# A fused attention and mixture-of-experts kernel: reordered prologue (second half's queries, a selector copy, a weight split, the load of batch 1)

## The reference, cut to what matters

```python
def block(x, ctx, g_xattn, g_ffn, weights):
    q = (layernorm(x) @ Wq.T).heads() / sqrt(16)
    k, v = (ctx @ Wk.T).heads(), (ctx @ Wv.T).heads()
    scores = q @ k.T + (q @ p_params)[clip(row - col, -4, 4) + 4]
    scores = where(row >= col, scores, -1e30)
    x = x + tanh(g_xattn) * (softmax(scores) @ v).merge() @ Wo.T
    x = x + tanh(g_ffn) * moe(layernorm(x))    # top 4 of 8 by groups, and a shared expert
    return x
```

## Time and profile before

| what | value |
|---|---|
| median of 3 runs | 638.78 us (636.84 to 639.2) |
| the profiled execution's own time | 637.0 us |
| its span, first to last instruction | 635.2 us |
| mean granted TensorE clock, share of full speed | 0.978 |
| TensorE matmul busy | 573.6 us, 90% of the span |
| VectorE busy | 420.9 us, 66% |
| ScalarE busy | 290.7 us, 46% |
| GpSimd busy | 197.0 us, 31% |

### The profile page before, as it was taken

How to read it: one execution, slowest core, us unless ns; L and a number is a source line. 1 busy time by engine, 2 the same in 40 slices (tenths; PEclk the granted TensorE clock), 3 DMA queues, 4 the chain that set the end, 5 groups by cost and what they waited for, 6 DMA issues and landing times.

```text
span 635.2 us, 10542 instructions
## 1 busy us (share of the span) xinstructions
PE 573.6 (90%) x3232; PEld 451.9 (71%) x3232; DVE 420.9 (66%) x884; ACT 290.7 (46%) x549; POOL 197.0 (31%) x199
## 2 busy tenths in 40 slices
PE   3647978899989999888989999999999999999997
PEld 3436745566557655544768888888888888888886
DVE  5396659875997688755777557466474754746454
ACT  3443578446855695477324342242423334233222
POOL 4155015500542045200123333224243242333223
PEclk9777999899999999999999999999999999999999
DMA  5883345435443535541510312203222032121320
GB/s 179 189 203 106 83 88 131 96 81 111 109 116 92 110 98 117 163 156 38 142 46 2 108 60 84 83 0 100 66 72 69 25 100 66 51 69 48 102 67 33
DMA packets 43585, 58.13 MB, mean 92 GB/s; under 512 B 8448, under 2 KB 25856, under 8 KB 43520
## 3 DMA queue, kind: packets, MB, share of 16 engines
q1 hardware_dynamic: 42464, 55.90, 32.4%
q10 hardware_dynamic: 1088, 1.84, 1.3%
HBM read 33.13 MB, written 6.11 MB: 62 GB/s over the span
## 4 chain that ended last, share of the span: by engine, by line
PE 74%; DVE 13%; issue 5%; ACT 3%; DMA 2%; SPq 1%; ACTq 1%; POOL 0%; DVEq 0%; POOLq 0%
PE py L1674 16%; PE pg L1658 16%; PE pu L1658 15%; PE smax L1010 4%; DVE mx L731 3%; PE oT L1077 3%; PE work L984 3%; PE work L1092 3%; PE oT L1081 3%; PE sT L1057 2%; DVE sx L746 2%; PE sT L1056 2%; PE pm L1628 1%; PE work L946 1%; PE pm L1620 1%
## 5 line engine op out<-in xcount | busy, mean ns | idle before, releaser
L1321 POOL TENSOR_TENSOR hl<-sg,hh 128x512 fp32r<-128x512 f32 x72 | 94.0, 1306 | 209.7 <-ACT hh L1366 209.7
L622 ACT ACTIVATE ex<-sT 128x512 f32<-128x512 f32 (+1 forms) x160 | 92.4, 593 | 75.1 <-PE sT L1057 53.3
L1360 ACT ACTIVATE sg<-pg 128x512 f32<-128x512 f32 x72 | 43.1, 598 | 181.6 <-PE pu L1658 181.5
L1674 PE MATMUL py<-split,hh 128*128 128x256 f32 x576 | 113.9, 282 | 0.1
L731 DVE TENSOR_REDUCE mx<-smax 128x2 f32<-128x308 f32 x187 | 81.1, 472 | 27.1 <-PE smax L1010 25.7
L1674 PEld LDWEIGHTS py<-split,hh 128*128 128x128 f32 x576 | 93.3, 189 | 3.9 <-issue 0.5
L1658 PE MATMUL pu<-x2h,split 128*128 128x512 f32 x288 | 90.5, 395 | 0.0
L1658 PE MATMUL pg<-x2h,split 128*128 128x512 f32 x288 | 90.3, 394 | 0.0
L1674 PE MATMUL py<-split,hl 128*128 128x256 f32 x288 | 80.6, 282 | 0.0
L1658 PEld LDWEIGHTS pu<-x2h,split 128*128 128x128 f32 x288 | 54.1, 188 | 13.0
L1500 DVE TENSOR_TENSOR sg<-cwb,sg 128x512 f32<-128x512 f32 x64 | 56.9, 891 | 8.9 <-DMA cwb<-cwt_d 6.3
(11 more groups left out here) (162 smaller groups left out, 953.1 us busy)
## 6 DMA issues: line engine op xcount, KB each, us to landing
cwb<-cwt_d SPq DMA_DIRECT2D x64, 256.0 KB, 3.4
qs<-qh SPq DMA_DIRECT2D x56, 128.0 KB, 2.5
ks<-km SPq DMA_DIRECT2D x16, 231.0 KB, 3.1
qs<-ql SPq DMA_DIRECT2D x28, 128.0 KB, 2.5
at<-rden_d SPq DMA_DIRECT2D x56, 64.0 KB, 2.3
out<-x SPq DMA_DIRECT2D x7, 512.0 KB, 4.5
wx<-in_wx SPq DMA_DIRECT2D x9, 384.0 KB, 7.4
x<-in_x SPq DMA_DIRECT2D x3, 1024.0 KB, 13.7
```

The lines of the kernel that those rows point to most:

```text
L622: nc.scalar.activation(ex[:, g % 2, i % 5, q0:HALF], ST[i % 2][:, q0:HALF], ACT.Exp).then_inc(exp_s, 1)
L1321: nc.gpsimd.tensor_tensor(hl[:, i % R, :], sg[:, i % R, :], hh[:, i % R, :], ALU.subtract).then_inc(hl_done, 1)
L1360: nc.scalar.activation(sg[:, i % R, :], PG[i % RG][:], ACT.Silu).then_inc(sg_s, 1)
L1674: return nc.tensor.matmul(PY[j // 2][:, (j % 2) * D:(j % 2 + 1) * D], ha[:, i % R, j * P:(j + 1) * P], wa[:, e, 2 * C * I:XW], start=first ...
```

## The change

Four pieces of the prologue change their place; no arithmetic is added or dropped.
- TensorE does the queries of half 1 after the 32 score products and `max_T` instead of ahead of them. `q_out` of half 1 (ScalarE), `q_lo` of half 1 (VectorE, after `tile0`) and the twelve DMAs of its rows follow. Each queue issues the four DMAs of the high parts once `q_hi` is 4, and the two of the low parts once `work_free` is 10.
- ScalarE's long selector copy goes between `x_hi` and `q_out` of half 0; the short ones go behind the `near` copies, and `m_row` goes ahead of `q_out` and `q_rows` of half 1.
- VectorE makes `wql` after the relative-position constants and the normalised x of half 0. TensorE's wait for `wq_set` stays where it is.
- SyncE issues the load of x of batch 1 ahead of the rows of half 1; those of batches 2 and 3 stay behind them.

```diff
--- before.py
+++ after.py
@@ -396,9 +396,11 @@
         sp.wait_ge(km_in, K_LOADS)
         for g in range(NG):
             k_stack(g)
-        sp.wait_ge(work_free, 9)
-        q_stack(1, 0)
         x_load(1)
+        sp.wait_ge(q_hi, 4)
+        q_stack(1, 0, (0, 2))
+        sp.wait_ge(work_free, 10)
+        q_stack(1, 0, (1,))
         for i in range(2, B):
             x_load(i)
         batches(sp, unit)
@@ -560,17 +562,20 @@
                                src[0:32, :, :].rearrange("p j d -> p (j d)").unsqueeze(1)
                                .broadcast_to([32, NSTK, 2 * DIST])).then_inc(const_set, 1)
 
-        def selectors():
+        def long_selectors():
 
             act.wait_ge(pool_set, 4)
+            nc.scalar.copy(ks[96:128, :, :].rearrange("p s (j k) -> p s j k", j=2),
+                           con("head", 96, 128).rearrange("p (s j) -> p s j", j=2).unsqueeze(3)
+                           .broadcast_to([32, NSTK, 2, KL])).then_inc(const_set, 1)
+
+        def short_selectors():
+
             for par in range(2):
                 nc.scalar.copy(k2[96:128, par::2, :].rearrange("p s (q k) -> p s q k", q=4)
                                [:, :, 2 * par:2 * par + 2, 0:K1],
                                con("head", 96, 128).rearrange("p (s j) -> p s j", j=2)[:, par::2, :].unsqueeze(3)
                                .broadcast_to([32, NG, 2, K1])).then_inc(const_set, 1)
-            nc.scalar.copy(ks[96:128, :, :].rearrange("p s (j k) -> p s j k", j=2),
-                           con("head", 96, 128).rearrange("p (s j) -> p s j", j=2).unsqueeze(3)
-                           .broadcast_to([32, NSTK, 2, KL])).then_inc(const_set, 1)
 
         def x_hi(u, use):
             for c in range(C):
@@ -652,20 +657,23 @@
         constants_late()
         k_hi(0, MAX_BANKS[0], True)
         x_hi(0, 0)
+        long_selectors()
         q_out(0, 2)
         act.wait_ge(work_free, 4)
         q_rows(act, 0, 1, range(3))
         x_hi(1, 5)
-        selectors()
+        for p in range(0, NM, 2):
+            near(0, p, M_START, True)
+        short_selectors()
+        for stk in range(1, NSTK):
+            m_row(0, 0, stk)
         for part in range(2):
             act.wait_ge(qs_in[0][part], 16 * 6)
-        q_out(1, 7)
-        for p in range(0, NM, 2):
-            near(0, p, M_START, True)
-        act.wait_ge(work_free, 9)
-        q_rows(act, 1, 1, range(3))
-        for stk in range(1, NSTK):
-            m_row(0, 0, stk)
+        q_out(1, 8)
+        act.wait_ge(q_hi, 4)
+        q_rows(act, 1, 1, (0, 2))
+        act.wait_ge(work_free, 10)
+        q_rows(act, 1, 1, (1,))
         batches(act, unit)
         raw_out(2 * B - 1, 1, 3)
 
@@ -876,8 +884,6 @@
         dve.wait_ge(x_first, 16)
         norm_stats(0, 0)
         dve.wait_ge(w_in, 5 * 16)
-        dve.wait_ge(wq_set, 1)
-        nc.vector.scalar_tensor_tensor(wql[:], wq, SCALE, wqh[:], ALU.mult, ALU.subtract).then_inc(wq_set, 1)
         nc.vector.tensor_scalar(reld[:], rel[:, DIST:2 * DIST], rel[:, 2 * DIST:], None, ALU.subtract)\
             .then_inc(rel_set, 1)
         dve.wait_ge(rel_set, 1)
@@ -888,6 +894,8 @@
         dve.wait_ge(rel_set, 2)
         nc.vector.tensor_tensor(rell[:], relm[:], relh[:], ALU.subtract).then_inc(rel_set, 1)
         normalised(0, 0, start=True)
+        dve.wait_ge(wq_set, 1)
+        nc.vector.scalar_tensor_tensor(wql[:], wq, SCALE, wqh[:], ALU.mult, ALU.subtract).then_inc(wq_set, 1)
         k_lo(0, MAX_BANKS[0])
         x_lo(0, 0)
         dve.wait_ge(x_in[0], 16)
@@ -896,15 +904,15 @@
         normalised(0, 1)
         v_in(0, 4, True)
         x_lo(1, 5)
-        q_lo(1, 7)
         for p in range(1, NM, 2):
             maximum(0, 0, p, M_START, True)
         minus_max(0, 0, start=True)
         tile1_add(0, True)
-        max_out(0, 0, 9, start=True)
+        max_out(0, 0, 7, start=True)
         tile1_max(0, 0)
         tile1_subtract(0)
         tile0(0, 0, True)
+        q_lo(1, 8)
         dve.wait_ge(x_in[1], 16)
         dve.wait_ge(g_set, 1)
         batches(dve, unit)
@@ -1131,7 +1139,6 @@
         pe.wait_ge(kv_in, 2 * 16)
         values_in(0, -1, START + 4)
         transposes(1, -1, START + 5)
-        queries(-1, START + 5, START + 7)
         pe.wait_ge(pool_set, 6)
         pe.wait_ge(const_set, 5)
         pe.wait_ge(km_in, K_LOADS)
@@ -1145,7 +1152,8 @@
                 if last >= 0:
                     pe.wait_ge((sx_s, mx_s)[last // 2 % 2], 2 * (last // 4) + last % 2 + 1)
                 stack_scores(first_tile(p), first_stack(p, k), M_START[q % len(M_START)])
-        max_T(0, 0, -1, START + 9)
+        max_T(0, 0, -1, START + 7)
+        queries(-1, START + 5, START + 8)
         pe.wait_ge(const_set, 8)
         batches(pe, unit)
         for short in range(2):
```

## The result

The changed kernel is slower: 641.91 us in the median of 20 runs (636.14 to 643.86), the kernel before 638.32 (636.30 to 640.19, 20 runs). The ratio is 1.0041 with a 95% interval of 1.0024 to 1.0058: +2.6 us (1.5 to 3.7; the medians themselves are 3.6 apart), just under the 3.2 us that I had called the limit of no change. The profiled execution lies at the slow end of its runs, 643.63 us for a span of 641.8, so it shows each wait at a large size; the ratio is the measure of the typical cost.

The account below looks back on a forecast made before the run. Prediction: TensorE, busy 90% of 635.2 us, carries any prologue shift through to the end. +0.2, +1.0 and +0.3 sum to +1.5 us: 638.5 like the profiled execution, 640.3 against the median; given 640.2, range 636.6 to 643.6.

Parts of the forecast that it names:

- part 6: TensorE's first product needing the rows of half 1: waits for their landing, +0.3 us, ends 0 and 3.3.
- Part 1: Prologue front: `wql` behind normalised x delays TensorE's first instruction from 8.39 to 11.3, +2.9 us.
- Parts 2 and 7: ScalarE's long selector copy in an idle gap, and SyncE's reordered loads of x: 0 each; loads' upper end +1.
- Part 3: Front of the maxima: moving half 1's queries gains 2.7 us at most, limited by row landing; first maximum +0.2.
- The rival of the slow clock at both places: First queries of half 0 and maxima both at the slow clock: 643.9 us, slower; chance 0.13.
- Part 4: Maxima: TensorE, idle before them, starts at 1.2 GHz; +1.0 us, between 0 and 2.3.
- third rival: Rows of half 1 late: TensorE stands at its first product of half 1, scores behind it; 642.5 us, chance 0.08.
- Part 5: Queries of half 1 behind `max_T`: fit TensorE's idle time before the scores; cost 0, at most 0.5 us.
- Shift s: Shift of the first score of unit 0, +1.5 us, carried undiminished to the kernel's end.

Follow-up runs that it names:

- rows_first: Changed kernel, but SyncE waits for the landing of the rows of half 1 before issuing x of batches 2 and 3; 1.0041 of the kernel before.
- wql_back: Changed kernel with the split of `wql` put back where it was; 1.0006 of the kernel before.
- kept_busy: Changed kernel with 24 unread matmuls into an unused bank behind the transposes of half 1; 1.0050 of the kernel before.
- wait_moved: Changed kernel with TensorE's wait for `wq_set` moved from the head of its program to the first queries; 1.0005 of the kernel before.

## Why the prediction was right or wrong

The sign and the class were right, and so was the mechanism at the front: 640.2 against 641.9 measured, within the range; +1.5 against +2.6 by the ratio (1.5 to 3.7). That the sum came this near is in part luck. At the first product with half 1 the kernels with this front and order were 3.1 (`rows_first`) to 3.8 us late (6.3 in the profiled execution of the changed kernel), about twice the 1.5 of the sum; the first score of unit 0, for which the sum without its last term, the 0.3 of part 6, foresaw +1.2, was 1.3 to 2.0 us late (2.6). What arrived at the end depends on the clock behind it. Step by step:

- **Part 1, the late split, +2.9 at the front.** Right, and the largest term: 2.6 in the trace, 1.7 alone, 2.2 undone. `rstd` took 1.02 us this time against 1.34, so normalised x started at 8.90 and the delay was 0.3 less. Moving the wait showed that it is the wait's place and not the split's that costs.
- **Parts 2 and 7, selectors and loads.** Right at nothing: 0.9992. The keys of batch 1 did not wait for their context.
- **Part 3, the landing is late next.** Right: the first product was released by the rows, at 31.01 against 30.6 foreseen. The first maximum came at 32.17, +0.7 against the +0.2 foreseen. The gain on the old schedule was over-sized: the rows were to be there at 27.7, `wql_back` has 28.54, 1.4 us ahead of 29.97 and not 2.3.
- **The rival of the slow clock at both places** came half true: in five of the six profiled executions with the late front (all but `kept_busy`) the first queries of half 0 ran at the low level, and the twelve took 4.3 to 4.9 us instead of 3.0. On the path to the rows this was worth little in the new order: `kept_busy`, where they took 3.0, has its first product at 30.55, against 30.82 in `rows_first`.
- **Part 4, slow maxima, +1.0.** Right in size for the typical execution (1.0 to 1.6 in five traces), and under-sized for the profiled one, where they took 9.4 against 7.3 us, +2.1, near the 2.3 of paying in full. The clock did rise within the maxima, as foreseen, but only by 40 in the profiled execution (0.51 from 31 to 40). What the slow maxima cost in time was not isolated.
- **Part 6, the rows of half 1, +0.3.** This is the step that failed. I took the landing of one issue in a quiet stretch, 2.4 us, "as this queue is empty now". The twelve copies of the two queues make the stretch crowded by themselves: 1.57 MB at 214 GB/s. The last took 6.2 us in the changed kernel and the wait was 3.4, my upper end 3.3; in the other traces of this queue order it was 1.6 to 2.1, still five times the term. It is the third rival's mechanism, though not for its reason: that the loads of x matter is not shown. I should have divided the bytes by the rate of the earlier trace rows (269 GB/s at most) instead of picking a latency.
- **Part 5, queries behind `max_T`, 0.** Right that they hold up nobody on TensorE. But at the low clock they end at 47.4, and all twelve copies wait for their last half; this is where the lateness of the rows begins.
- **Shift s carried through undiminished.** Wrong for the single execution. In `rows_first` the first product with half 1 is 3.1 us later than before, and the span only 0.1 longer (635.3). The clock behind it makes the difference. Two stretches of the units, each from one position in TensorE's program to another, first of the kernel before, then of `rows_first`:

```profile
61.00:81.00 20.00, 18.95 (x120) 14.43 (x120) 13.28 (x31) 9.27 (x18) 3.08 (x3) 0.91 0.34 80
110.80:146.00 35.20, 31.79 (x199) 22.55 (x200) 28.63 (x62) 17.70 (x37) 10.51 (x11) 0.95 0.40 95
```

```profile
64.50:83.00 18.50, 17.31 (x121) 12.86 (x120) 13.37 (x31) 9.69 (x19) 2.84 (x3) 1.00 0.37 86
112.70:146.40 33.70, 30.14 (x199) 21.79 (x199) 28.70 (x62) 17.57 (x37) 10.50 (x11) 1.00 0.45 106
```

The same work takes 1.5 us less in each, where the clock has no low stretch, and so the 3.1 us are gone by 146. In the profiled execution of the changed kernel 4.9 to 5.5 of its 6.3 us are left from 116 to 248, and 1.5 more come at the low stretch by 277.

## What to carry to other kernels

A wait at the head of an in-order engine's program makes everything on it late; when a producer is moved behind other work, move its wait down to its first reader in the same edit. Work taken off the front of a stage only brings what the next input leaves: here the rows landed 1.4 us ahead of the old start (28.54 against 29.97, `wql_back`), and the burst of twelve copies landed by its bytes over the DMA rate, not by the latency of one. To get an input sooner, let both queues issue the half that is needed first before the other: 26.0 instead of 28.5 here. And before reading a wait off one trace, look at it in a second kernel that shares the stage.

## What the runs showed of the hardware that was not expected

In the new order the mean granted clock is lower. In the 35 runs of before that go with the first four experiments it had a median of 0.977; in the 12 each of `wql_back`, `rows_first` and `wait_moved`, which all have the new order, it was 0.969 to 0.970. Within each of these kernels a longer time went with a lower clock (correlations of 0.76 to 0.78 between the time and the time spent at the low level, 0.23 to 0.36 us of time for each us at it). This is not proof that the clock sets the time: the mean counts stretches in which TensorE stands idle, and `kept_busy`, whose added matmuls fill one, has 0.976 and is no faster. Nor do all kernels of the new order scatter more: the 20 runs of the changed kernel spread over 7.7 us and those of before over 3.9, but 12 of `wql_back` over 3.1, and the 35 of before over 6.0.

Some of the low stretches come long after the prologue. The changed kernel (641.8 us), whose clock from 58 to 130 was 0.90 as shown above, and then `rows_first` (635.3 us), which is the same up to the place of two loads:

```profile
260.00:280.00 20.00, 16.40 (x95) 12.03 (x94) 13.00 (x31) 9.24 (x18) 3.96 (x4) 0.91 0.73 232
```

```profile
58.00:130.00 72.00, 64.39 (x369) 43.80 (x370) 57.38 (x116) 45.05 (x93) 25.71 (x28) 0.96 0.46 115
260.00:280.00 20.00, 16.96 (x101) 11.35 (x97) 14.42 (x39) 10.91 (x21) 1.53 (x3) 1.00 0.66 220
```

Why the order of the prologue should show there is not explained by these runs; that in the new order TensorE stands for a longer time in the prologue and starts the units at the low level would fit, and was not tested apart. What one low stretch costs can be read from the two pairs of stretches in the section before. 35.2 us at a mean of 0.95 hold some 3.5 us at the low level (an estimate: twice the 0.05 that is missing, times the length), and they took 1.5 us longer than the same 199 matmuls at 1.00; so each microsecond at the low level cost some 0.4 there.

Where the clock has no record, the view shows 1.00: in the stretch 14 to 20 of the changed kernel it does, while the first queries took 0.63 us each, the length of the low level. There the length of an instruction is the better witness. (The records of that execution begin with the rise at about 19.3.)
